# Audio tower on one core: queues written out, gathered rows weighted in one instruction, and another order of pieces

## The chip, the core and the metric

The kernel runs on one core of a Trainium2 chip. A core has TensorE (PE, matmuls into eight PSUM banks), VectorE (DVE), ScalarE (ACT), GpSimd (POOL) and SyncE (SP), each with its own instruction queue and in order; they wait for one another by semaphores. 16 DMA engines move data between HBM and the on-chip SBUF. The metric is the device time of one execution in microseconds (us).

## What is computed

128 sequences of 750 x 64 floats go through a deformable tokenizer (16 taps a word, each read at a computed fractional position), one attention with an additive tanh score, and a mixture of 8 experts of which 2 count, plus a shared expert. Cut to what matters here:

```python
off = jnp.einsum('bwkc,ock->bow', xr, w_off) + b_off[None, :, None]
dy, dx = off[:, 0::2], off[:, 1::2]
px = base[None] + dx;  x0 = jnp.floor(px);  frac = px - x0
wy = jnp.maximum(0.0, 1.0 - jnp.abs(dy))
val = wy[:, None] * ((1.0 - frac)[:, None] * v0 + frac[:, None] * v1)   # v0, v1: rows x0 and x0 + 1
out = jnp.einsum('bckw,dck->bwd', val, w_def) + b_def                    # + class token, positions
h = h + attention(layernorm(h))       # scores + W2 . tanh(hq + hk + b1), softmax
h = h + experts(layernorm(h))         # top 2 of 8, relu, and a shared expert
```

## The kernel before

Work goes in 16 units of 8 sequences. In each unit six sequences take their rows by 36 indirect DMAs of POOL (`gathers`, L382, 128 rows each) into `G`; the other two are read densely: ACT makes hat weights `HT` (pieces `h0`..`h3` for the first of the two, `k0`..`k3` for the second: three Abs instructions of 128x736 at L413, then one Relu of 128x2208 at L420, for each half), and PE multiplies them with the rows `XN` (pieces `n0`..`n3`, L818). Both meet in `VT`, which `b3` (L779) multiplies with the tokenizer's weights.

Each engine's program is a list of short names, `ORDER`; one pass through it is a step. `AHEAD` says how many units ahead of the step a piece works: `t` (turning x, L535) 4 units ahead, `a3`/`a4` (offsets: matmul L793, ACT copy L404, matmul L800, then `stage_a` on DVE from L543) 3 ahead, `h` 2, `k`, `n`, `c`, `b` 1, `m` 0 (first layernorm and attention), `r` one behind (softmax, second layernorm, router), `f`, `g`, `d`, two behind (experts). Expert e is `fe` (PE L940, then ACT relu `HE` L494), `ge` (PE L951 spreads its weight into bank 3, DVE multiplies `GE` L728) and `de` (PE L963). Bank 0 is shared in turn by `a3`, `a4`, `n0` to `n3` and `b3`; bank 2 holds one `f` at a time, bank 3 one `g`.

`c0`, `c1`, `c2` (`combine`, L597 to L618) weight the gathered rows: for each third of a unit a product of 128x768 in place for the first row of every pair, then twice a product of 128x384 into PSUM bank 1 (`prod`) and a sum of 128x384 into `VAL`, and a transpose into `VT`. `stage_a` makes the positions and the indices (`idx`, which POOL waits for) and then, still on DVE, the weights `nw`, `e01` and `aw`. `rstd` is three Newton rounds of three small instructions; `m13` ranks the experts. POOL and SP run their middle part in hardware loops; POOL waits for `idx_ready` of a unit and for `g_free`, counted up by `combine`, before it fills one of two `G` buffers again. SP's list is `x0` (next x), `e0 e1` (the estimates of the tanh score out to HBM), `e2` (back, regrouped, into `SC`, which `r6` of the next step reads), `p0`, `q0` (positions out and back), `y0` (`XN`), `d9` (the store).

## Time and profile before

| | before |
|---|---|
| median of 3 runs | 860.05 us (859.48 to 864.42) |
| the profiled execution | 864.31 us |
| its span, first to last instruction | 862.5 us |
| PE busy | 691.1 us (80%) |
| DVE busy | 670.7 us (78%) |
| ACT busy | 515.8 us (60%) |
| POOL busy | 547.7 us (63%) |
| mean granted TensorE clock | 0.956 |

Busy time is the sum of an engine's instructions; the waits between them are not in it. POOL's gathers have a fixed gap ("issue") between them that is not counted as busy either. The chain that ended last puts 41% of the span on DVE and 37% on PE.

### The profile page before, as it was taken

To read this page: it belongs to the slowest core of one execution; us is meant where nothing else is said; L and a number is where in the kernel's file an instruction comes from. 1 tells how busy PE (TensorE), PEld (TensorE's weight loads), DVE (VectorE), ACT (ScalarE), POOL (GpSimd) and SP (SyncE) were. 2 spreads that over 40 slices of the span, in tenths; PEclk is the share of its full clock that TensorE was granted. 3 is DMA by queue.
4 is the path that set the end of the run, shared out by engine and by line. 5 is a ranking of instruction groups with operands and counts; after the bars stand their busy time and mean duration, and the time that the engine had idled before them with its cause. 6 is when DMAs were issued, how large, how long until landed. Compare 5 with 4: busy or idle time off the path is not lost.

```text
span 862.5 us, 17862 instructions
## 1 busy us (share of the span) xinstructions
PE 691.1 (80%) x6294; PEld 416.1 (48%) x6294; DVE 670.7 (78%) x1750; ACT 515.8 (60%) x903; POOL 547.7 (63%) x588
## 2 busy tenths in 40 slices
PE   2106586879899898989898988888888999998786
PEld 0004354545465555555464645555554555555342
DVE  5146667879888988898898989898888889796552
ACT  0217565647675857767576758585775767744422
POOL 1777777777777777777777777777777777300000
PEclk9999978899989998999999999999999999999889
DMA  4877486647373747565564647475756354200101
GB/s 145 183 180 192 88 170 137 125 84 176 58 206 61 186 86 154 118 123 143 100 169 57 197 76 170 101 155 117 138 131 125 73 93 99 44 18 10 27 0 19
DMA packets 130669, 97.79 MB, mean 113 GB/s; under 512 B 87180, under 2 KB 118868, under 8 KB 130588
## 3 DMA queue, kind: packets, MB, share of 16 engines
q1 hardware_dynamic: 111292, 58.64, 26.3%
q0 software_dynamic: 18432, 37.79, 25.7%
q8 instruction: 50, 0.82, 0.4%
q10 hardware_dynamic: 864, 0.30, 0.1%
q14 instruction: 31, 0.25, 0.1%
HBM read 88.75 MB, written 7.90 MB: 112 GB/s over the span
## 4 chain that ended last, share of the span: by engine, by line
DVE 41%; PE 37%; issue 9%; ACT 5%; SPq 4%; DMA 3%; DVEq 0%; ACTq 0%
PE bank L779 8%; PE bank L940 6%; PE bank L818 5%; DVE XT L535 4%; PE bank L963 4%; DVE bank L609 4%; DVE VAL L615 4%; PE bank L854 3%; DVE G L606 3%; DVE TH L654 3%; DVE VT L632 3%; PE bank L793 2%; DVE GE L728 2%; ACT HT L413 2%; SPq L288 2%
## 5 line engine op out<-in xcount | busy, mean ns | idle before, releaser
L382 POOL DMA_INDIRECT G<-in_x,idx x576 | 545.4, 947 | 195.7 <-issue 173.7
L413 ACT ACTIVATE HT<-PXB,c_lneg 128x736 f32<-128x736 f32 x192 | 160.1, 897 | 74.4 <-PE bank L818 55.5
L818 PE MATMUL bank<-HT,XN 128*32 128x184 f32 x3072 | 137.9, 329 | 8.5 <-ACT HT L420 5.2
L940 PE MATMUL bank<-Z,c_w1e 128*128 128x376 f32 x288 | 125.9, 519 | 20.3 <-ACT HE L494 18.4
L420 ACT ACTIVATE HT<-HT 128x2208 f32<-128x2208 f32 x64 | 130.3, 2036 | 0.6
L818 PEld LDWEIGHTS bank<-HT,XN 128*32 128x32 f32 x3072 | 102.8, 113 | 42.7 <-issue 17.5
L779 PE MATMUL bank<-VT,c_wdef 128*128 128x380 f32 x256 | 87.2, 495 | 23.2 <-DVE VT L632 23.2
L963 PE MATMUL bank<-GE,c_w2e 128*128 128x376 f32 x256 | 104.4, 513 | 0.7 <-DVE GE L728 0.7
L535 DVE STREAM_TRANSPOSE XT<-xt 128x768 f32<-128x768 f32 x64 | 59.9, 958 | 54.2 <-DMA xt<-in_x 33.3
L494 ACT ACTIVATE HE<-bank,c_fb 128x376 f32<-128x376 f32 x128 | 73.0, 570 | 38.9 <-PE bank L940 37.2
L728 DVE TENSOR_TENSOR GE<-HE,bank 128x376 f32<-128x376 f32 x128 | 68.7, 537 | 34.4 <-ACT HE L494 24.7
L779 PEld LDWEIGHTS bank<-VT,c_wdef 128*128 128x128 f32 x256 | 48.1, 193 | 61.5 <-DVE VT L618 28.5
L940 PEld LDWEIGHTS bank<-Z,c_w1e 128*128 128x128 f32 x288 | 49.7, 193 | 57.4 <-ACT HE L494 31.4
L963 PEld LDWEIGHTS bank<-GE,c_w2e 128*128 128x128 f32 x256 | 45.1, 198 | 31.5 <-issue 17.5
L609 DVE TENSOR_TENSOR bank<-G,bank 128x384 f32<-128x384 f32 x96 | 54.0, 562 | 3.3
L615 DVE TENSOR_TENSOR VAL<-G,bank 128x384 f32<-128x384 f32 x96 | 53.1, 553 | 3.3
L793 PE MATMUL bank<-XT,c_wof 128*32 128x384 f32 x256 | 26.5, 536 | 30.3 <-DVE XT L535 20.3
L463 ACT ACTIVATE SC<-SC,smx 47x47 f32<-47x47 f32 x128 | 40.8, 320 | 16.5 <-DVE smx L667 16.5
L618 DVE STREAM_TRANSPOSE VT<-VAL 128x768 f32<-128x768 f32 x48 | 47.0, 978 | 1.7
L606 DVE TENSOR_TENSOR G<-G,bank 128x768 f32<-128x768 f32 x48 | 45.4, 945 | 0.6
L951 PE MATMUL bank<-cT,selb 72*128 72x376 bf16 x128 | 43.5, 340 | 0.3 <-DVE GE L728 0.2
L834 PE MATMUL bank<-h,c_center 128*128 128x376 f32 x64 | 29.1, 536 | 16.7 <-DVE smx L667 16.7
(136 smaller groups left out, 931.3 us busy)
## 6 DMA issues: line engine op xcount, KB each, us to landing
xt<-in_x SPq DMA_DIRECT2D x256, 96.0 KB
PXB<-pw SPq DMA_DIRECT2D x16, 768.0 KB
G<-in_x,idx POOLq DMA_INDIRECT x576
XN<-in_x SPq DMA_DIRECT2D x16, 384.0 KB
est<-SQHC SPq DMA_DIRECT2D x32, 141.0 KB
WYB<-pw SPq DMA_DIRECT2D x64, 48.0 KB
out<-OUTS SPq DMA_DIRECT2D x64, 44.0 KB
SC<-est SPq DMA_DIRECT2D x16, 69.0 KB
```

Of the source, the lines that this page charges most:

```text
L382: pool.indirect_dma_start(out=G[h][:, col, :], out_offset=None, in_=x.rearrange("b (l c) -> (b l) c", c=C), in_offset=bass.IndirectOffsetO ...
L413: act.activation(HT[half][:, c, :, :].rearrange("p g (w n) -> p g w n", n=4), PXB[h][:, :].rearrange("p (g w i n) -> p i g w n", g=NG, i=2 ...
L420: act.activation(rows_, rows_, ACT.Relu, bias=1.0, scale=-1.0).then_inc(hat_ready, 1)
L494: act.activation(HE[e % 4][:, :], cols(2), ACT.Relu, bias=cs["fb1"][:, e:e + 1]).then_inc(he_ready, 1)
L535: dve.transpose(XT[:, :, 96 * bp:96 * bp + 96].rearrange("p q (t i) -> p t q i", i=32), xt[:, WG * bp:WG * bp + WG, :].rearrange("p t (q i ...
L609: ins = dve.tensor_tensor(prod, G[h][:, k0 + a:k0 + b, C:2 * C], weight(1, a, b), ALU.mult)
L615: chain(dve.tensor_tensor(VAL[:, a:b, :], G[h][:, k0 + a:k0 + b, 0:C], prod, ALU.add))
L728: dve.tensor_tensor(GE[e % 4][:, :], HE[e % 4][:, :], cols(3), ALU.mult).then_inc(ge_ready, 1)
L779: mm = pe.matmul(bank[0][:, 0:TOK], wdef[:, q, :], VT[:, q, :], start=(q == 0), stop=(q == KP - 1))
L818: mm = pe.matmul(bank[0][32 * g:32 * g + 32, HW * c:HW * c + HW], XN[h][:, b, C * ch + 32 * c:C * ch + 32 * c + 32], HT[half][:, k, g, :], ...
L940: pe.matmul(cols(2), w1e[:, e, :], Z2[h][:, :], start=True, stop=True).then_inc(up_full, 1)
L963: pe.matmul(cols(4), w2e[:, e, :], HS[:, 0:COLS] if e == E else GE[e % 4][:, :], start=(e == E), stop=False).then_inc(down_done, 1)
```

## The change

- `combine`: one product of 128x1536 in place over both rows of every pair, then one sum of 128x768 that reads both halves of `G` from SBUF and writes `VAL`. The PSUM scratch `prod` is gone; the weights are multiplied out into `awp` at `c0`.
- `stage_a`: the bias of the offsets is added by ACT in `a3`. Abs and Relu that make `nw` and `e01` go to ACT as a new piece `a4` (`row_hats`, five small instructions), `nw` and `e01` are doubled, and the positions are written by SP after ACT's piece.
- `rstd`: 7 small instructions for 9. `m13`: one comparison for two. `m6`: the maximum comes out negated, one instruction less. `dense_out`: a product without the factor -1.
- `ORDER` is another one on all four engines. SP's `y0` stands ahead of `e0 e1 e2`, and `q0` behind the store.
- The loops of SP and POOL are written out. At the start x of unit 0 is issued half by SP and half by ACT, the first constants by POOL ahead of its memsets, the other constants by ACT behind step -3.

```diff
-    "tensor": ("gc n0 fs g0 n1 m0 f0 ds f1 m1 r7 f2 g1 r8 d0 m2 g2 r9 m3 f3 g3 m4 r10 m5 f4 g4 m51 d1 r11 f5 n2 g5 m52 n3 "
-               "r12 d2 f6 g6 d3 b3 f7 g7 a3 d4 a4 d5 d6 d7 d8").split(),
+    "tensor": ("n0 fs gc g0 n1 f0 ds m0 f1 m1 r7 d0 g1 f2 r8 m2 g2 f3 m3 r9 g3 m4 d1 r10 m5 f4 m51 d2 g4 f5 m52 r11 g5 n2 "
+               "f6 r12 g6 d3 f7 g7 d4 d5 n3 d6 b3 d7 d8 a3 a4").split(),
...
-    "sync": ("x0 e0 e1 e2 p0 q0 y0 d9").split(),
+    "sync": ("x0 y0 e0 e1 e2 p0 d9 q0").split(),
...
+        def load_first(eng, parts):
+
+            for bp in parts:
+                src = x[bass.ds(2 * bp, 2), :].rearrange("b (t w g n) -> g w b t n", t=WG, w=16, g=NG)
+                for g in range(NG):
+                    eng.dma_start(xt[32 * g:32 * g + 32, WG * bp:WG * bp + WG, :], src[g]).then_inc(x_in[bp], 16)
...
-            load_x(0, 0)
+            load_first(sp, (0, 1))
...
+            for name, _s in CONSTS[1:NFIRST]:
+                pool.dma_start(cs[name][:, :], consts[name]).then_inc(first_in, 16)
+            pool.dma_start(ident[:, :], consts["ident"]).then_inc(ident_in, 16)
...
-            gathers(0, 0)
-            gathers(0, 1)
-            with pool.Fori(1, UNITS // 2) as i:
-                gathers(i, 0)
-                gathers(i, 1)
+            for u in range(UNITS):
+                gathers(u // 2, u % 2)
...
-                act.activation(off4[:, :], bank[0][:, 0:XCOLS], ACT.Copy).then_inc(off_ready, 1)
+                act.activation(off4[:, :], bank[0][:, 0:XCOLS], ACT.Identity, bias=cs["boff"][:, 0:1]).then_inc(off_ready, 1)
+
+            def row_hats(m, h):
+                u = 2 * m + h
+                act.wait_ge(ot_read, u + 1)
+                if not (isinstance(m, int) and u < 2):
+                    act.wait_ge(pw_out, 6 * 16 * (u - 1))
+                act.activation(nw[h][:, :, :], offT[:, :, 0:4], ACT.Abs).then_inc(nw_abs, 1)
+                act.wait_ge(nw_abs, u + 1)
+                act.wait_ge(rest_ready, u + 1)
+                act.activation(nw[h][:, :, :], nw[h][:, :, :], ACT.Relu, bias=1.0, scale=-1.0).then_inc(pw_ready, 1)
+                for i in range(2):
+                    act.activation(e01[h][:, :, :, i], rest[:, :, :], ACT.Abs, bias=float(i)).then_inc(e_abs, 1)
+                act.wait_ge(e_abs, 2 * u + 2)
+                e = e01[h][:, :, :, :].rearrange("p t n s -> p (t n s)")
+                act.activation(e, e, ACT.Relu, bias=1.0, scale=-1.0).then_inc(e_ready, 1)
...
+            for name, _s in CONSTS[NFIRST + 1:]:
+                act.dma_start(cs[name][:, :], consts[name]).then_inc(const_in, 16)
...
-                chain(dve.scalar_tensor_tensor(nw[:, :, :], offs[:, :, 0:4], -1.0, offs[:, :, 0:4], ALU.mult, ALU.max))
-                dve.tensor_scalar(nw[:, :, :], nw[:, :, :], 1.0, 1.0, ALU.min, ALU.subtract).then_inc(pw_ready, 1)
-                dve.wait_ge(pw_ready, u + 1)
-                chain(dve.scalar_tensor_tensor(e01[:, :, :, 0], rr[:, :, :], ROUND, pxg, ALU.subtract, ALU.subtract))
-                chain(dve.tensor_scalar(e01[:, :, :, 1], e01[:, :, :, 0], 1.0, None, ALU.add))
-                chain(dve.scalar_tensor_tensor(e01f, e01f, -1.0, e01f, ALU.mult, ALU.max))
                 chain(dve.tensor_scalar(rowb[:, :], rowb[:, :], float(NB * LP), None, ALU.add))
-                chain(dve.tensor_scalar(e01f, e01f, 1.0, 1.0, ALU.min, ALU.subtract))
-                chain(dve.tensor_tensor(aw[h][:, :, :, :], e01[:, :, :, :],
-                                        nw[:, 0:GBLK, :].unsqueeze(3).broadcast_to([128, GBLK, 4, 2]), ALU.mult))
...
-                    first = G[h][:, k0:k0 + 2 * n, 0:C]
-                    chain(dve.tensor_tensor(first, first, weight(0, 0, 2 * n), ALU.mult))
-                    for part in range(2):
-                        a, b = n * part, n * part + n
-                        ins = dve.tensor_tensor(prod, G[h][:, k0 + a:k0 + b, C:2 * C], weight(1, a, b), ALU.mult)
...
-                        chain(dve.tensor_tensor(VAL[:, a:b, :], G[h][:, k0 + a:k0 + b, 0:C], prod, ALU.add))
+                    n = 4 * WG
+                    pairs = G[h][:, k0:k0 + n, :].rearrange("p k (s c) -> p k s c", s=2)
+                    chain(dve.tensor_tensor(pairs, pairs, awp[:, k0:k0 + n, :].unsqueeze(3).broadcast_to([128, n, 2, C]), ALU.mult))
+                    dve.tensor_tensor(VAL[:, :, :], pairs[:, :, 0, :], pairs[:, :, 1, :], ALU.add).then_inc(g_free, 1)
+                    dve.wait_ge(g_free, GP * u + bp + 1)
```

What moves on PE is shown where one step passes into the next, which the prediction calls the seam. Before: `b3`'s matmul (L779) stands two rows ahead of the first of these; `a3` (L793) and `a4` (L800) stand among experts' matmuls, then come `gc` (L929) and `n0` (L818).

```order
L951 MATMUL bank<-cT,selb 128x376
L793 MATMUL bank<-XT,c_wof 32x384 x8
L963 MATMUL bank<-GE,c_w2e 128x376
L800 MATMUL bank<-off,c_selm 128x384
L963 MATMUL bank<-GE,c_w2e 128x376 x3
L968 MATMUL bank<-cT,b2s 128x376
L929 MATMUL bank<-identb,c 72x94 x4
L818 MATMUL bank<-HT,XN 32x184 x24
L940 MATMUL bank<-Z,c_w1e 128x376
L951 MATMUL bank<-cT,selb 128x376
L818 MATMUL bank<-HT,XN 32x184 x24
```

In the changed kernel, the same place (line numbers are its own: L736 is `b3`, L920 a `d`, L925 `d8`, L750 `a3`, L757 `a4`, L775 an `n`, L897 an `f`, L886 `gc`, L908 a `g`):

```order
L775 MATMUL bank<-HT,XN 32x184 x24
L920 MATMUL bank<-GE,c_w2e 128x376
L736 MATMUL bank<-VT,c_wdef 128x380 x8
L920 MATMUL bank<-GE,c_w2e 128x376
L925 MATMUL bank<-cT,b2s 128x376
L750 MATMUL bank<-XT,c_wof 32x384 x8
L757 MATMUL bank<-off,c_selm 128x384
L775 MATMUL bank<-HT,XN 32x184 x24
L897 MATMUL bank<-Z,c_w1e 128x376
L886 MATMUL bank<-identb,c 72x94 x4
L908 MATMUL bank<-cT,selb 128x376
L775 MATMUL bank<-HT,XN 32x184 x24
```

`a3` and `a4` now stand side by side with nothing behind them before `n0`, and `g0` comes directly behind `gc`; `n3` stands right ahead of `b3` but for one `d`.

On ACT, at the end of a step, the kernel before had these rows (L457 the estimates, L420 and L413 the hats, L476 the router's Exp, L494 an expert's relu, L404 `a3`, L481 `gc`):

```order
L457 ACTIVATE SQHC<-bank 128x282
L420 ACTIVATE HT<-HT 128x2208
L476 ACTIVATE eg<-lg 94x32
L413 ACTIVATE HT<-PXB,c_lneg 128x736 x3
L494 ACTIVATE HE<-bank,c_fb 128x376
L420 ACTIVATE HT<-HT 128x2208
L494 ACTIVATE HE<-bank,c_fb 128x376
L404 ACTIVATE off<-bank 128x384
L481 ACTIVATE cT<-bank 72x376
```

and the changed kernel these (L447 the router's Exp, L391 and L384 the hats, L465 a relu, L360 `a3`, L367 to L375 the new `a4`, L452 `gc`):

```order
L447 ACTIVATE eg<-lg 94x32
L391 ACTIVATE HT<-HT 128x2208
L384 ACTIVATE HT<-PXB,c_lneg 128x736 x3
L391 ACTIVATE HT<-HT 128x2208
L465 ACTIVATE HE<-bank,c_fb 128x376
L384 ACTIVATE HT<-PXB,c_lneg 128x736 x3
L391 ACTIVATE HT<-HT 128x2208
L360 ACTIVATE off<-bank,c_boff 128x384
L367 ACTIVATE nw<-offT 128x48
L370 ACTIVATE nw<-nw 128x48
L372 ACTIVATE e<-rest 128x36 x2
L375 ACTIVATE e<-e 128x72
```

Five of the eight hat pieces (`k3`, `h0` to `h3`) now stand together ahead of `a3`, with one relu between them.

## Rows read from the trace of the kernel before

**Rows 1.** Busy time by stretch: us, busy of each engine, clock, DMA share, GB/s

```profile
225.03:649.97 424.94, 378.47 (x3539) 230.52 (x3538) 371.01 (x974) 287.99 (x504) 321.30 (x341) 0.97 0.59 128
```

**Rows 2.** Timeline: offT of units 3 and 15, one `c2`

```profile
132.95 0.54 DVE L543 STREAM_TRANSPOSE offT<-bank 128x384 f32<-128x384 f32 x1
696.29 0.58 DVE L543 STREAM_TRANSPOSE offT<-bank 128x384 f32<-128x384 f32 x1 [2.72 <-PE bank L800]
...
767.74 0.94 DVE L606 TENSOR_TENSOR G<-G,bank 128x768 f32<-128x768 f32 x1
```

**Rows 3.** Waits of PE from 411.6 to 459.2: us in total, times, longest

```profile
PE bank L779 <- DVE VT L632: 1.5, 1, 1.5
PE bank L793 <- DVE h L643: 1.3, 2, 0.6
PE bank L834 <- DVE smx L667: 1.2, 1, 1.2
PE bank L940 <- ACT HE L494: 1.0, 1, 1.0
```

**Rows 4.** Timeline of POOL: the first gather and the last of unit 15

```profile
22.42 1.09 POOL L382 DMA_INDIRECT G<-in_x,idx  x1 [19.59 <-DVE idx L551]
...
742.95 0.94 POOL L382 DMA_INDIRECT G<-in_x,idx  x1 [0.30 <-issue]
```

**Rows 5.** Groups by line and form: count, busy us, mean ns, idle before

```profile
L535 DVE STREAM_TRANSPOSE XT<-xt 128x768 f32<-128x768 f32 x64 | 59.9, 958 | 54.2 <-DMA xt<-in_x 33.3 <-PE bank L793 20.5 <-DVE aw L563 0.2
L609 DVE TENSOR_TENSOR bank<-G,bank 128x384 f32<-128x384 f32 x96 | 54.0, 562 | 3.3
L615 DVE TENSOR_TENSOR VAL<-G,bank 128x384 f32<-128x384 f32 x96 | 53.1, 553 | 3.3
L606 DVE TENSOR_TENSOR G<-G,bank 128x768 f32<-128x768 f32 x48 | 45.4, 945 | 0.6
L577 DVE TENSOR_TENSOR diag<-c_ident,ry 94x376 f32<-94x376 f32 x32 | 17.5, 546 | 1.1
L574 DVE SCALAR_TENSOR_TENSOR nt_<-ry 94x4 f32<-94x4 f32 x96 | 15.5, 161 | 3.3
```

**Rows 6.** One `stage_a` from its second instruction, by stretch: us, DVE busy (x)

```profile
415.67:419.08 3.41, 2.99 (x13) 1.00 0.24 61
```

**Rows 7.** Groups by line and form on ACT, and two on PE

```profile
L413 ACT ACTIVATE HT<-PXB,c_lneg 128x736 f32<-128x736 f32 x192 | 160.1, 897 | 74.4 <-PE bank L818 55.5 <-DMA PXB<-pw 18.9
L420 ACT ACTIVATE HT<-HT 128x2208 f32<-128x2208 f32 x64 | 130.3, 2036 | 0.6
L494 ACT ACTIVATE HE<-bank,c_fb 128x376 f32<-128x376 f32 x128 | 73.0, 570 | 38.9 <-PE bank L940 37.2 <-DVE GE L728 1.3
L463 ACT ACTIVATE SC<-SC,smx 47x47 f32<-47x47 f32 x128 | 40.8, 320 | 16.5 <-DVE smx L667 16.5
L818 PE MATMUL bank<-HT,XN 128*32 128x184 f32 x3072 | 137.9, 329 | 8.5 <-ACT HT L420 5.2 <-DVE offT L543 2.6 <-ACT w1pad L515 0.7
L940 PE MATMUL bank<-Z,c_w1e 128*128 128x376 f32 x288 | 125.9, 519 | 20.3 <-ACT HE L494 18.4 <-ACT HS L487 1.8
```

**Rows 8.** Timeline: estimates out and in on SP, and a late read

```profile
448.22 1.06 SPq L326 DMA_DIRECT2D est<-SQHC  x2
454.91 0.28 SPq L333 DMA_DIRECT2D SC<-est  x1
806.71 0.27 SPq L333 DMA_DIRECT2D SC<-est  x1
812.64 0.60 DVE L665 SCALAR_TENSOR_TENSOR SC<-bank,c_b2col,SC 47x376 f32<-47x376 f32 x1 [1.36 <-DMA SC<-est]
```

**Rows 9.** Timeline of the start on SP: x of unit 0, the first late constant

```profile
0.76 10.41 SPq L288 DMA_DIRECT2D xt<-in_x  x16
33.55 0.48 SPq L351 DMA_DIRECT2D c_wdef<-in_wdef  x1
```

**Rows 10.** Timeline of DVE: `c2` of unit 1

```profile
117.58 0.92 DVE L606 TENSOR_TENSOR G<-G,bank 128x768 f32<-128x768 f32 x1
```

More of the change, by code:

```diff
@@ L348, in _ @@
                       "e0": write_estimate(0), "e1": write_estimate(1), "e2": read_estimate}
-            early("sync", pieces, -3)
-            for name, _s in CONSTS[NFIRST + 1:]:
-                sp.dma_start(cs[name][:, :], consts[name]).then_inc(const_in, 16)
-            sp.wait_ge(zeroed, 1)
-            for b in range(NB):
-                sp.dma_start(w2blk[H * b:H * b + H, b:b + 1], rows["w2col"]).then_inc(blk_in, 16)
-            early("sync", pieces, -2)
-            steps(sp, "sync", pieces, last=(UNITS - 6) // 2)
+            steps("sync", pieces, -3, UNITS + 2)
             for h in range(2):
@@ L769, in _ @@
             dve.wait_ge(zeroed, 8)
-            steps(dve, "vector", pieces, chain, loop=False)
+            steps("vector", pieces, -1, UNITS + 2)
         @block.tensor
@@ L991, in _ @@
             pe.wait_ge(setup_mats, 5)
-            steps(pe, "tensor", pieces, loop=False)
+            steps("tensor", pieces, 0, UNITS + 2)
 def kernel(**inputs):
```

156 lines of the change are left out of this document (58 added, 98 removed).

## Prediction, written before the changed kernel was run

> **What bounds the kernel now.** I read the busy time by stretch first. In the nine steps from `offT` of unit 5 to that of unit 14 a step takes 424.94 / 9 = 47.2 us; PE is busy 378.47 / 9 = 42.05 of it, DVE 41.2, ACT 32.0 [rows 1]. No engine is full: PE stands idle 5.2 us a step, and a step cannot go under 42 without less PE work, of which the change takes none. The chain in the table ahead (DVE 41%, PE 37%) says that the two hand the work to and fro.
>
> Next, PE's waits in one step [rows 3]: 1.5 in `b3` for the last transposed row, 1.3 in `a3` for `h0`, 1.2 in `m0` for the softmax maxima (DVE had to get there), 1.0 in `f1` for ACT's relu. Those four are 5.0 of the 5.2. The first three, 4.0 us, are DVE being late, and this is what a lighter DVE can give back.
>
> Then POOL, which its 63% hides. The first gather starts at 22.42 and the last at 742.95 [rows 4]; 575 gathers between them make 720.5 / 575 = 1.253 us each, 45.1 a unit, with next to no waiting. So POOL is a second bound: the last third of unit 15 cannot be combined before its start + 722 and some landing. `c2` of unit 15 runs at 767.74 now [rows 2], 24 us behind POOL's last start. With a step of 47.2 against POOL's 45.1, POOL has slack late in the run; a step under 45.1 would buy nothing more.
>
> **DVE's part.** `combine`: 562 ns against 945 ns for 384 and 768 columns is 1.0 ns a column [rows 5], so the product of 1536 takes 0.945 + 0.77 = 1.71, the sum of 768 0.95, together 2.66 against 0.945 + 2 x 0.562 + 2 x 0.553 = 3.18. With two gaps less it saves 0.6 a third, 1.8 a unit. `stage_a`: 13 instructions in 3.41 [rows 6], of which six stay: 1.8 less. `rstd`: twice two instructions of 0.161 and their gap of 0.03, 0.8. `m13` and `m6`: one instruction of 256 columns (0.4 by the same 1.0 ns a column) and one small, 0.6. Sum: 5.0 of DVE's 41.2 a step, 80 us over 16 units. The bound from below for the sum with both inputs in SBUF is the 0.553 x 2 of today's halves; from above I come to it as a rival.
>
> **ACT's part.** Five small instructions a unit, each between 0.16 (L574) and 0.32 (L463) [rows 5, 7]: 1.2. ACT had 15 us to spare a step. They stand behind `a3`, where ACT would wait for `gc` anyway; `gc` gets its turn about 2.5 after `offT`, when PE reaches it too. I cost them at nothing; were PE not still in `n0`, it would be up to 1.2 a step.
>
> **The step after.** DVE's 5.0 only counts where PE waits for DVE, so I go through PE's waits in the new order, with durations of the rows.
> 1. `a3`, `a4`, `n0` follow each other on bank 0, and no expert's matmul covers them any more (the seam in the order rows). After `a3`, ACT copies (0.5, like L494's 0.57 [rows 7]) and `a4` follows; after `a4`, DVE transposes (0.54 [rows 2]) and `n0` follows. With 0.15 of latency each, an estimate: 0.7 + 0.7 = 1.4.
> 2. `g0` comes directly behind `gc` and waits for ACT's copy of `cT`: 0.5.
> 3. `f1` waits for ACT's relu of `f0`, which is behind the eight Exps of `r6`. From the end of `offT`: the rest of `stage_a` 1.6, four transposes 4 x 0.958 less overlap = 3.7 [rows 5], sum and maximum 1.2, eight Exps at 0.32 = 2.6, relu 0.57 [rows 7]: 9.7. PE has `n0 fs gc g0 n1 f0 ds m0` in it: two dense pieces at 137.9 / 64 = 2.15, four of the size of L940 at 125.9 / 144 = 0.87 less 0.15 of overlap each [rows 7], `gc`, `g0` and the 0.5 of point 2: 8.1. Wait 1.6.
> 4. `f2` waits for the relu of `f1`, which ACT does behind `k0` (3 x 0.897 less overlap = 2.4 [rows 7]) and two copies: 3.6 after `f1` starts, PE has 2.9 in it: 0.7.
> 5. `b3` waits for `dense_out` of `n3` (0.8 and latency) with one `d` beside it: 0.3.
> 6. From `f2` to `n3` I find PE with work throughout: DVE, 5 us lighter, reaches `diag`, `GE` and `VT` ahead of it.
>
> Sum 4.5 against 5.2 today. So the reordering and the lighter DVE remove the waits for `VT`, `h0` and the maxima, and lay bare a seam that was covered. A step becomes 42.05 + 4.5 = 46.5, 0.7 less. The twelve steps from `offT` of unit 3 (132.95) to unit 15 (696.29) [rows 2] give 8.4.
>
> **Start.** x of unit 0 takes SP 10.41 us for 16 issues [rows 9]; on two queues it is there some 5 earlier. But DVE also waits for the first constants, and POOL issues them now, six at about a gather's 1.25: 7.5 and the landing, which eats a part of the 5. Unit 0's offsets then no longer stand behind x of unit 1. I take the first gather at 20.3 (18.5 if POOL's issues are quick, 22 if slow). The constants that began at 33.55 on SP [rows 9] are issued by ACT from about 21, and x of unit 2 is not behind them. So the setup comes ten earlier and POOL becomes the limit: `c2` of unit 1 no earlier than 20.3 + 72 x 1.253 + 1.5 = 112, now 117.58 [rows 10]. I take 6 for the start.
>
> **End.** Behind unit 15's offsets the steps are chains of latency; two `rstd` (0.4 each), one ranking, one `combine` and a maximum lie on them, and DVE reaches the softmax sooner: 3, with 0 and 6 as bounds, as the order of pieces changes too.
>
> **Sum.** 6 + 8.4 + 3 = 17.4. The profiled execution took 864.31, which is 0.5% over the median of 860.05; 864.3 - 17.4 = 846.9, times 860.05 / 864.31 is 843.
>
> **Rivals.**
> - *POOL is the limit (chance 0.18).* If the waits of points 3 and 4 are shorter, the step falls to 45.1 and POOL never stops. `c2` of unit 15 then comes at 20.3 + 722 + 1.5 = 744, 24 earlier, and 3 at the end: 837, or 833. For it: DVE has 11 us a step to spare. Against: points 3 and 4 are ACT's chain, not DVE's.
> - *The step gains nothing (0.22).* ACT has five hat pieces in a row ahead of `a3`: three Relus of 2.0, two triples of 2.4 and a relu, 11.5 [rows 7], against 13 on PE from `g6` to the end of `a3`. 1.4 of slack; if ACT comes to `k3` 2 later than I think, each step is 0.7 longer and stays at 47.2. The same comes out if the estimate is late: `y0` now holds SP until `dense_out` of this step, so `e0`, `e1`, `e2` follow it; issue to issue 6.7, and 5.9 from `e2` to the sum that waits for it [rows 8], 13.5 with `y0`, against 15 until `r6`. Only start and end are left: 864.3 - 9 = 855, or 851 to 858.
> - *The sum from memory to memory disturbs POOL (0.07), slower.* Today each large product or sum of `combine` has one side in PSUM. If each new sum of 0.95 holds up one gather, or waits for one, POOL needs 45.1 + 3 x 0.95 = 48.0 a unit; its last gather starts at 788, `c2` of unit 15 at 790 for 767.74: 864.3 + 22 - 3 = 883, or 879. It decides from 2.2 us a unit on. Against it: `diag` has both inputs in SBUF, and its 546 ns for 376 columns lie on the same line as the products with PSUM (0.562 for 384) [rows 5], and POOL's pace of 1.253 leaves no room for held gathers [rows 4]. The Trainium skill (SBUF — State Buffer, Who interferes with whom) says that a DVE instruction with two SBUF inputs contends with a GpSimd instruction that reads SBUF, and only with such a one; the gather reads its indices there. By that rule the time is this rival's; the rows of today do not show it.
> - *The seam is dearer (0.05).* Should `a3` to `n0` cost 3.5 in place of 1.4, the step is 48.6: 864.3 - 9 + 17 = 872, or 868.
>
> **Chances.** The forecast (838 to 850) has 0.48. Faster by over 1%, about what a measurement of this kernel can tell, is under 851.4: the forecast, POOL's case and a third of the no-gain case, with a little off for what I have not seen, 0.70. Within 1%: 0.19. Slower: 0.11, the last two rivals. The range from 832 to 859 holds the first three cases.
>
> **What would show it.** `offT` to `offT` in the middle: 46.5 (45.1 for POOL, 47.2 for no gain). DVE busy down to about 590. The product of 1536 at 1.71, the sum at 0.95; POOL's gather still 0.947 and its gap 0.3. First gather at 18.5 to 22. PE's waits for ACT at `f1` and `f2`, and for `off` and `offT` at the seam, in place of those for `VT`, `h` and `smx`. Wrong I would be if PE's busy time moved, if DVE waited for gathers in the middle of the run, or if SP's estimate ended a wait in every step.

## The result and the profile after

| | before | after |
|---|---|---|
| median of 4 executions | 862.23 us (859.48 to 865.72) | 852.97 us (846.73 to 856.24) |
| the profiled execution | 864.31 us | 846.73 us |
| `offT` of unit 0 to that of unit 3 | 113.2 us | 112.7 us |
| twelve steps, `offT` of unit 3 to that of unit 15 | 563.3 us | 552.9 us |
| `offT` of unit 15 to the end | 166.2 us | 160.1 us |

The ratio is 0.989 (0.986 to 0.992): 1.1% faster, where 2.0% was forecast. The profiled execution of the changed kernel is the quickest of its four, that of before one of its slower ones; the pair differs by 17.6 us, the medians by 9.3. The table's last three rows are read from the two profiled executions.

Busy time, from the page of the changed kernel:

```profile
PE 692.2 (82%) x6294; PEld 407.5 (48%) x6294; DVE 607.0 (72%) x1399; ACT 534.9 (63%) x983; POOL 562.6 (67%) x594
```

DVE is down by 63.7 us (80 forecast), PE as it was, POOL up by 15. Nine steps by stretch, to be set beside [rows 1]:

```profile
224.31:639.20 414.89, 378.07 (x3537) 222.45 (x3537) 336.57 (x774) 298.44 (x549) 315.23 (x328) 0.98 0.67 129
```

and PE's waits in the same stretch (us in total, times, longest):

```profile
PE bank L897 <- ACT HE L465: 14.9, 14, 2.2
PE bank L757 <- ACT off L360: 6.8, 9, 0.8
PE bank L775 <- DVE offT L520: 6.1, 9, 0.7
PE bank L908 <- ACT cT L452: 5.1, 9, 0.6
PE bank L736 <- DVE VT L594: 2.3, 9, 0.3
```

A step is 414.89 / 9 = 46.1 us, 1.1 less than in [rows 1]; over the twelve steps of the table it is 46.08 for 46.95, 0.9 less. PE is busy 42.0 of it as before, and its waits have changed places: those of [rows 3] for `h` and `smx` and most of that for `VT` are gone; in their place stand the seam (`off` 0.76, `offT` 0.68), the copy `cT` 0.57, and ACT's relu 1.66 a step.

POOL's group of gathers (count, busy, mean ns, idle before them and what ended it):

```profile
L343 POOL DMA_INDIRECT G<-in_x,idx x576 | 556.9, 967 | 190.0 <-issue 174.3 <-DVE idx L527 15.1 <-DVE VAL L576 0.6
```

and, to be set beside [rows 4], its first two gathers and its last one:

```profile
21.53 1.01 POOL L343 DMA_INDIRECT G<-in_x,idx  x1 [14.76 <-DVE idx L527]
22.84 0.98 POOL L343 DMA_INDIRECT G<-in_x,idx  x1 [0.30 <-issue]
...
752.73 0.94 POOL L343 DMA_INDIRECT G<-in_x,idx  x1 [0.30 <-issue]
```

Of 190.0 us idle between gathers, 174.3 are the 0.30 of issue and 14.8 the wait before the first. POOL never stops otherwise. From first to last it needs 731.2 / 575 = 1.272 us a gather, for 1.253 before: a gather takes 967 ns on average, 947 before. The last third of units 1 and 15 on DVE ([rows 10] and [rows 2] of before):

```profile
115.59 1.75 DVE L575 TENSOR_TENSOR G<-G,bank 128x1536 f32<-128x1536 f32 x1 [3.21 <-DMA G<-in_x,idx]
756.38 1.75 DVE L575 TENSOR_TENSOR G<-G,bank 128x1536 f32<-128x1536 f32 x1 [0.64 <-DMA G<-in_x,idx]
```

and the shares of the chain that ended last:

```profile
POOL 39%; PE 22%; issue 15%; DVE 8%; DMA 7%; ACT 7%; SPq 2%; POOLq 0%; ACTq 0%; DVEq 0%
```

In both places DVE waits for a gather. Before, the last third of unit 15 ran 24.8 us behind the start of POOL's last gather; now it runs 3.7 behind it, and POOL leads the chain where DVE and PE did.

One thing has to be said for what follows: on several of the later occasions every execution with all the gathers issued one behind the other, of the kernel before too, took near 1570 us; a section further down shows what happens in them. r1 to r10, r15 and r16 were measured on such occasions, r11 to r14, r17 and r18 on others, where the kernel before took near 862. A ratio is always to the kernel before on the same chip and occasion.

### The profile page after: what moved, and what is told of

Same layout as the page of the kernel before. It is cut to its first block, busy times and chain, and to the rows that moved or that the text cites. A ratio compares the mean times of both kernels' runs of the same rounds, so it can differ in the third digit from the quotient of the medians.

```text
span 844.9 us, 17031 instructions
## 1 busy us (share of the span) xinstructions
PE 692.2 (82%) x6294; PEld 407.5 (48%) x6294; DVE 607.0 (72%) x1399; ACT 534.9 (63%) x983; POOL 562.6 (67%) x594
## 4 chain that ended last, share of the span: by engine, by line
POOL 39%; PE 22%; issue 15%; DVE 8%; DMA 7%; ACT 7%; SPq 2%; POOLq 0%; ACTq 0%; DVEq 0%
POOL G L343 39%; PE bank L736 4%; PE bank L897 4%; PE bank L775 3%; PE bank L920 3%; ACT HT L384 2%; ACT SC L434 2%; DVE XT L511 2%; DMA SC<-est 1%; DMA est<-SQHC 1%; DMA G<-in_x,idx 1%; DMA PXB<-pw 1%; SPq L253 1%; ACT HT L391 1%; PE bank L869 1%
## 5 line engine op out<-in xcount | busy, mean ns | idle before, releaser
L343 POOL DMA_INDIRECT G<-in_x,idx x576 | 556.9, 967 | 190.0 <-issue 174.3
L384 ACT ACTIVATE HT<-PXB,c_lneg 128x736 f32<-128x736 f32 x192 | 159.8, 897 | 28.0 <-DMA PXB<-pw 21.9
L775 PE MATMUL bank<-HT,XN 128*32 128x184 f32 x3072 | 139.8, 334 | 24.4 <-DVE offT L520 9.4
L897 PE MATMUL bank<-Z,c_w1e 128*128 128x376 f32 x288 | 128.8, 530 | 28.0 <-ACT HE L465 26.6
L775 PEld LDWEIGHTS bank<-HT,XN 128*32 128x32 f32 x3072 | 98.5, 114 | 71.0 <-DVE offT L520 18.6
L391 ACT ACTIVATE HT<-HT 128x2208 f32<-128x2208 f32 x64 | 130.4, 2038 | 1.2
L465 ACT ACTIVATE HE<-bank,c_fb 128x376 f32<-128x376 f32 x128 | 72.6, 567 | 69.9 <-PE bank L897 52.8
L920 PE MATMUL bank<-GE,c_w2e 128*128 128x376 f32 x256 | 106.0, 510 | 0.0
L736 PE MATMUL bank<-VT,c_wdef 128*128 128x380 f32 x256 | 87.2, 495 | 9.4 <-DVE VT L594 9.4
L575 DVE TENSOR_TENSOR G<-G,bank 128x1536 f32<-128x1536 f32 x48 | 84.0, 1750 | 5.4 <-DMA G<-in_x,idx 4.8
L897 PEld LDWEIGHTS bank<-Z,c_w1e 128*128 128x128 f32 x288 | 47.9, 195 | 72.2 <-ACT HE L465 46.0
L736 PEld LDWEIGHTS bank<-VT,c_wdef 128*128 128x128 f32 x256 | 48.3, 193 | 47.6 <-issue 14.3
L511 DVE STREAM_TRANSPOSE XT<-xt 128x768 f32<-128x768 f32 x64 | 57.1, 947 | 1.3 <-DMA xt<-in_x 0.7
L520 DVE STREAM_TRANSPOSE offT<-bank 128x384 f32<-128x384 f32 x16 | 9.3, 583 | 66.3 <-PE bank L757 66.3
L920 PEld LDWEIGHTS bank<-GE,c_w2e 128*128 128x128 f32 x256 | 43.9, 193 | 24.7 <-issue 13.8
L908 PE MATMUL bank<-cT,selb 72*128 72x376 bf16 x128 | 42.8, 334 | 9.1 <-ACT cT L452 9.1
L576 DVE TENSOR_TENSOR VAL<-G 128x768 f32<-128x768 f32 x48 | 46.1, 960 | 1.6
L750 PE MATMUL bank<-XT,c_wof 128*32 128x384 f32 x256 | 26.5, 536 | 23.3 <-DVE XT L511 20.4
L757 PE MATMUL bank<-off,c_selm 128*128 128x384 f32 x32 | 15.3, 563 | 36.8 <-ACT off L360 36.8
```

Source lines behind the costliest of these rows:

```text
L343: pool.indirect_dma_start(out=G[h][:, col, :], out_offset=None, in_=x.rearrange("b (l c) -> (b l) c", c=C), in_offset=bass.IndirectOffsetO ...
L384: act.activation(HT[half][:, c, :, :].rearrange("p g (w n) -> p g w n", n=4), PXB[h][:, :].rearrange("p (g w i n) -> p i g w n", g=NG, i=2 ...
L391: act.activation(rows_, rows_, ACT.Relu, bias=1.0, scale=-1.0).then_inc(hat_ready, 1)
L465: act.activation(HE[e % 4][:, :], cols(2), ACT.Relu, bias=cs["fb1"][:, e:e + 1]).then_inc(he_ready, 1)
L511: dve.transpose(XT[:, :, 96 * bp:96 * bp + 96].rearrange("p q (t i) -> p t q i", i=32), xt[:, WG * bp:WG * bp + WG, :].rearrange("p t (q i ...
L575: chain(dve.tensor_tensor(pairs, pairs, awp[:, k0:k0 + n, :].unsqueeze(3).broadcast_to([128, n, 2, C]), ALU.mult))
```

## The experiments

Two theories stood against each other. **A**: POOL with its 576 gathers sets the changed kernel's time, and the new sum from SBUF to SBUF makes the gathers longer. **B**: the engines' own step sets it (seam and ACT's chain, as the forecast has it), and POOL stays hidden.

### r1: the changed kernel again

> The changed kernel once more, to see what its executions have in common. Its profiled execution took 846.7, three others 852.7 to 856.2. Theory A (POOL is the limit of this kernel, and how long its gathers are held varies from one execution to the next): the median is 852 to 853, and a second profile shows POOL without a stop from 21.5 on, with gathers longer than 0.95 us beside the sum L576, mean 960 to 985 ns; the longer the gathers in all, the longer the time. Theory B (the engines' step is the limit and the gathers merely keep up): the gathers take the same 556.9 us in all, or another sum that the time does not follow, and combine waits for no gather.

1568.39 us, 0.9986 of the kernel before (0.9962 to 1.001), which itself took 1572.17. Neither the times nor the 1.1% of the first measurement came back; POOL's mean gather was 958 ns. What executions of this kind can tell is how a change weighs in the part of a step that doesn't stand still.

### r2 and r5: the combine of before

Told in short (the names are the kernel's, the lines are not its own words):

```diff
-pairs = pairs * awp                       # one product, 1536 columns, in place
-VAL = pairs[..., 0, :] + pairs[..., 1, :]  # one sum, both inputs in SBUF
+first = first * w0                        # 768 columns
+for part in range(2):
+    prod = second[part] * w1              # 384 columns, into PSUM bank 1
+    VAL[part] = first[part] + prod        # 384 columns
```

> The changed kernel with the five products and sums of the kernel before in combine (one side of each large one in PSUM), all else as changed. DVE gets 0.5 to 0.6 us a third more, 1.8 a unit, of the 11 it has to spare. Theory A (the sum with both inputs in SBUF holds POOL's gathers, and POOL is the limit): the gathers go back to 945 to 950 ns, the last starts about 11 us earlier, and the time falls by 4 to 9 us against the changed kernel, to 844 to 849. Theory B (the step of PE, DVE and ACT is the limit): the time stays at 853 or rises by what the 1.8 us lay on the path, up to 858.

> The changed kernel with the five products and sums of the kernel before in combine, on another chip if it is given: in the four runs ahead of this one every execution of every kernel, that of before too, took 1565 to 1596 us, with ACT standing still for about 45 us once a step (12 such waits, 546 us), so they can't tell the theories apart. Theory A (the sum with both inputs in SBUF holds POOL's gathers, and POOL is the limit): gathers back to 945 to 950 ns, 844 to 849 us against 853 of the changed kernel. Theory B (the step of PE, DVE and ACT is the limit): 853 to 858.

1.0121 of before (1.0094 to 1.0148), and on another chip 1.0098 (1.0081 to 1.0115): by these ratios 1.4% and 1.1% over r1. Gathers fell to 952 and 950 ns. There DVE's own time is what counts, and the shorter gathers give nothing back. The old combine in the new order was not measured with all gathers near 862.

### r3: SP's read of rows later

```diff
-    "sync": ("x0 y0 e0 e1 e2 p0 d9 q0").split(),
+    "sync": ("x0 e0 e1 e2 y0 p0 d9 q0").split(),
```

> The changed kernel with y0 (the load of XN) moved on SP from ahead of e0 e1 e2 to behind them. The changed kernel's r6 waited 8.2 us in all for the estimate to come back. If those waits lie on the path (the step is the limit): 3 to 6 us faster than the changed kernel, 847 to 850. If POOL is the limit (theory A), the middle of the run gains nothing, and only the waits of the last two steps (3.3 and 1.9 us) can: 850 to 853. The waits of L627 for the estimate are to vanish in the middle either way.

0.9998 (0.9979 to 1.0018), r1's time. That the estimate comes too late behind `y0` is not what a step is made of. In the first profile too DVE waited for it only six times, 8.2 us in all.

### r4: the kernel before with the new order

The four lists of `ORDER` of the changed kernel in the kernel before (ACT's without `a4`, a piece it doesn't have there).

> The kernel before with the four lists of the changed kernel and nothing else (its stage_a stays whole on DVE, so ACT's a4 is left out). Prediction's account (the lighter DVE is needed for the new order: with DVE 5 us heavier, stage_a and four transposes stand at the seam ahead of r6, so the wait of f1 grows by 1.8 and r6 by as much): a step of 48 to 49 us, 862 to 885, slower than before. Rival (the order alone carries the gain): 850 to 856, as the changed kernel.

1.0111 of before (1.0084 to 1.0138): in executions of this kind the new order by itself makes the kernel before slower.

### r6: the sum twice

```diff
+chain(dve.tensor_tensor(VAL, pairs[:, :, 0, :], pairs[:, :, 1, :], ALU.add))
 dve.tensor_tensor(VAL, pairs[:, :, 0, :], pairs[:, :, 1, :], ALU.add).then_inc(g_free, 1)
```

> The changed kernel with the sum L576 issued twice (the second writes the same values again): 0.96 us more of DVE a third, 2.9 a unit, all of it with both inputs in SBUF. Theory A (that sum holds POOL's gathers): the time that gathers of over 1.0 us have beyond 0.944 doubles, and the mean gather goes from 967 to about 980 ns; where POOL is the limit the time is 6 to 11 us above the changed kernel. Theory B (the gathers are held by something else): the gathers stay at 967, and the time rises by 0 to 8 us from DVE's 2.9 a unit alone.

1.0116 (1.0079 to 1.0154), 1.3% over r1. 46 us more of DVE cost some 20 us of time; the mean gather went from 958 to 962 ns only. In these executions the engines mostly stand still while gathers are issued, so sum and gather seldom meet (29 gathers of r6 overlap a sum, 70 in the changed kernel's first profile). This run does not tell the two theories apart.

### r7 to r9: three gathers a unit

```diff
-for k in range(4 * WG):     # 12 gathers in each third
+for k in range(1):
```

> The changed kernel with one gather in each third of a unit in place of twelve (48 in all for 576). G is zeroed once by POOL and the combine runs on it at full size, so the output is not the reference's; DVE, ACT, PE and SP have all their work. On the chips of r1 to r6 ACT and PE stand still some 45 us a step while POOL issues its 36 gathers. Theory G (it is the gathers that hold them): with three gathers a unit the standstills go, the time falls from about 1570 to about 850. Theory other (clock or something else of those chips): it stays above 1400. If the gathers go, the step shows the engines' own limit. Theory A (POOL is what limits the changed kernel's step of 46.1): the step falls below 45.1, to 44 to 45 us, and the time to 820 to 835. Theory B (the seam and ACT's chain limit it): the step stays at 46.0 to 46.3 and the time at 840 to 850.

> The kernel before with one gather in each third of a unit in place of twelve, G zeroed once, all other work kept; output not the reference's. Theory G: the standstills go and the time falls to about 860. POOL had slack in the kernel before (step 46.95 for 45.1 of gathers), so both A and B expect 46.7 to 47.0 a step and 855 to 862. Against r7 theory B expects a ratio of 0.98 to 0.99 (what was measured with all gathers, 0.989), theory A 0.955 to 0.97.

> As r7, with the order of pieces of the kernel before (a4, which ACT must run, behind a3). Output not the reference's. Separates the order from the lighter instructions in the engines' own step. If the order of the change is what turns DVE's 5 us into a shorter step, this one is slower than r7 by 0.5 us a step or more, 6 us and up. The forecast's points 1 and 2 put 1.9 us of new waits on the new order and took 4.0 us of old ones away by the lighter DVE alone, which by itself would make this one faster than r7, by up to 1.5 a step. I expect r9 slower than r7 by 1%, as r4 showed the orders to matter by that much.

The kernel before took 1566.99 beside them. r7: 854.1 us. r8: 879.9. r9: 839.5. So the gathers are what makes the 1570: with one in twelve left, the time halves. And r9, the changed kernel's instructions in the order of before, is 1.7% quicker than r7, where 1% slower was expected. Even three gathers still held ACT: in nine steps of r8 and of r9,

```profile
ACT HT L417 <- remote: 45.0, 9, 5.1
```

```profile
ACT HT L388 <- remote: 37.3, 9, 4.4
```

("remote" is a releaser that the trace can't name), so the ratio of r7 to r8 is no clean answer to A or B. That needed kernels with no gather at all.

### r10: POOL pauses ahead of each third

```diff
+if u or bp:
+    q = GP * u + bp - 1     # the third before this one
+    pool.wait_ge(gathered[q // GP % 2][q % GP], 16 * 4 * WG * (q // GP // 2 + 1))
```

> The changed kernel, but POOL waits ahead of each third (twelve gathers) until the third before has landed, a pause of 3.6 to 4 us each, 11 to 12 a unit; nothing left out. Theory G1 (ACT and PE are held as long as gathers follow each other without stop, from the first on): they get on with their work in each pause, the standstill of 45 us breaks into three of 12 to 15, and the time stays within 2% of r1's 1568. Theory G2 (they are held only once a number of gathers is under way): the pause takes that away and the time falls by 200 us or more. Theory N (the pause doesn't let them go on): 12 x 11 us more, 1700.

1390.1 us, 0.886 of before (0.883 to 0.890). A step fell from 93.0 to 82.0 us although POOL now stands still until every twelve gathers have landed. G2 wanted 200 us or more, 177 came. ACT's standstills in one step, from its timeline:

```profile
572.02 0.57 ACT L468 ACTIVATE HE<-bank,c_fb 128x376 f32<-128x376 f32 x1 [8.92 <-remote]
581.38 0.48 ACT L419 ACTIVATE Y<-bank 128x376 f32<-128x376 f32 x1 [8.79 <-remote]
...
589.14 0.60 ACT L409 ACTIVATE V<-bank 128x512 f32<-128x512 f32 x1 [4.79 <-remote]
```

One of 45 us has become several of 5 to 9. Pauses let PE and ACT on.

### r11 to r14: no gathers

`G` is zeroed once, POOL issues nothing, all the rest of the work stays.

> The changed kernel with no gathers at all: G is zeroed once by POOL and the combine runs on it at full size; all the work of DVE, ACT, PE and SP is kept, the output is not the reference's. Three gathers a unit still left PE 11.2 us of holes without a releaser in nine steps of r7 (1.2 a step) and ACT 13.5; these should go. Theory A (POOL and its gathers set the changed kernel's step): 44.9 to 45.2 a step. Theory B (the engines set it, gathers cost nothing): 46.0 to 46.4. The time is then 830 to 840 or 845 to 855.

> The kernel before with no gathers, G zeroed once, all other work kept; output not the reference's. In r8 ACT stood 45.0 us at the hats with a releaser that the trace does not show, 5.0 a step, and PE 11.1 behind it; without gathers this goes. The engines' own step of the kernel before, expected at 46.9 by both theories (it had 1.8 us of slack to POOL's 45.1), time 855 to 865; ratio r11 / r12 by B 0.985 to 0.99, by A 0.96 to 0.975.

> The changed kernel's instructions in the order of the kernel before, no gathers; output not the reference's. By r9 against r7 (839.5 and 854.1) the new order costs 1.7%. If that came from where the held instructions stand and not from the order as such, r13 equals r11 within 0.3%. If the order itself costs, r13 is 0.5 to 1 us a step quicker, 830 against 845. I expect the latter, with a step of 45.0.

> The changed kernel with the combine of before (four halves, products through a PSUM bank), no gathers; output not the reference's. DVE is 1.8 us a step dearer. With all gathers it was 1.3% slower than the changed kernel (r2, and 1.1% by r5). If that is DVE's own time on the path, it is so here too: 0.8 to 1.3% over r11. If the combine only counted through the gathers (held ones, or G freed later), it is within 0.3% of r11.

The kernel before took 861.19 beside them.

| no gathers | time, us | ratio to before (with its gathers) | step, mean of 12 |
|---|---|---|---|
| r12 kernel before | 853.4 | 0.9892 (0.9858 to 0.9927) | 46.64 |
| r11 changed kernel | 843.8 | 0.9791 (0.9753 to 0.9829) | 45.66 |
| r14 changed kernel, old combine | 863.5 | 1.0016 (0.9991 to 1.0042) | 46.67 |
| r13 changed kernel, old order | 798.8 | 0.9265 (0.9235 to 0.9294) | 42.66 |

None of the four is quite what had been expected: r11's step lies between A's 44.9 to 45.2 and B's 46.0 to 46.4, r12 is just under its 855 to 865, r13 was put at 830 us, and r14 is 2.3% over r11 for 0.8 to 1.3 expected.

The same nine steps, by stretch and then PE's waits. r11:

```profile
226.01:635.34 409.33, 375.37 (x3537) 220.90 (x3537) 333.33 (x775) 298.54 (x549) 0.00 (x0) 0.99 0.31 79
```

```profile
PE bank L895 <- ACT HE L463: 12.4, 17, 0.8
PE bank L755 <- ACT off L358: 6.8, 9, 0.8
PE bank L773 <- DVE offT L518: 6.1, 9, 0.7
PE bank L906 <- ACT cT L450: 5.1, 9, 0.6
PE bank L734 <- DVE VT L592: 2.3, 9, 0.3
```

r13:

```profile
207.99:593.58 385.59, 369.51 (x3539) 227.23 (x3538) 327.93 (x775) 294.24 (x549) 0.00 (x0) 0.99 0.33 84
```

```profile
PE bank L895 <- ACT HE L463: 8.9, 9, 1.0
PE bank L748 <- DVE h L603: 5.7, 9, 0.6
PE bank L836 <- DVE TH L614: 0.7, 3, 0.2
```

Four things follow. (1) Changed kernel against kernel before: 843.8 / 853.4 = 0.989 without gathers, as with them, and a step is 1.0 us shorter for 0.9 with them. The engines' own step carries most of the difference, as B says; by the medians the gathers cost both kernels some 9 us. The times are a little unfair to r11, r13 and r14: with `G` being zeroed, their first `offT` comes at 23.5 us, for 19.2 in the changed kernel and 19.8 in r12. The steps don't have this flaw. (2) All of the change but the order (r13 against r12) takes 4.0 us off a step and 55 off the time. (3) Without gathers the new order gives 3.0 of those 4.0 and 45 of the 55 us back. Its five waits are 32.7 / 9 = 3.6 us a step where the old order leaves 15.3 / 9 = 1.7, and PE's busy time in r13 is 0.65 a step lower. (4) The in-place combine is worth 1.0 a step and, by the medians, 20 us in this order, for 1.3 us of DVE's busy time a step (11.7 us in the nine steps, r14 against r11).

### r15 and r17: the changed kernel with the old order, all gathers

```diff
-    "tensor": ("n0 fs gc g0 n1 f0 ds m0 f1 m1 r7 d0 g1 f2 ...
-               "... f7 g7 d4 d5 n3 d6 b3 d7 d8 a3 a4").split(),
+    "tensor": ("gc n0 fs g0 n1 m0 f0 ds f1 m1 r7 f2 g1 ...
+               "... d3 b3 f7 g7 a3 d4 a4 d5 d6 d7 d8").split(),
```

(The other three lists likewise, with `a4` behind `a3` for ACT.)

> The changed kernel with the order of pieces of the kernel before (a4, which ACT must run, behind a3); all 576 gathers, nothing left out. Without gathers this order made a step of 42.66 us against 45.66 of the changed kernel (r13, r11). If the executions are of the kind of the first measurement (kernel before near 862): theory A, POOL is the limit as soon as the engines are quicker: POOL starts at about 21.5 and issues 576 gathers at 1.25 to 1.27, so its last third lands at 745 to 757, 86 to 88 us of tail follow, 832 to 845 in all, and a step is 45.1 to 45.8 with DVE waiting for gathers. Theory B, gathers cost the engines no time: 42.7 to 43.5 a step is impossible beyond POOL's pace, so it would show only as 835 and DVE never waiting. In either case faster than before by 2 to 3.5%. If they are of the kind of r1 (near 1570): 1540 to 1560, as the new order alone cost 1.1% there (r4).

> The kernel of r15 once more (changed kernel, order of pieces of the kernel before, nothing left out), because r15 and its kernel before ran near 1570. If the kernel before is near 862 here: by theory A 832 to 845, 0.965 to 0.98 of it, with DVE waiting for gathers at the first third of most units and a step of 45.1 to 45.8; if the gathers left no trace the 42.66 of r13 would give 800, which POOL's 576 gathers at 1.25 rule out. If the kernel before is near 1570 again: 0.987 as r15.

r15: 0.987 (0.984 to 0.990) beside executions near 1570. r17, with the kernel before at 862.1: 856.8 us, 0.9934 (0.9901 to 0.9966). Faster than before, but above the 0.965 to 0.98 that A had given, and no quicker than the changed kernel (0.989, measured on another occasion): with all gathers the new order gives nothing back. Of the 55 us that this order had without gathers 5 are left. The chain that ended last, and two groups, of r17:

```profile
POOL 55%; issue 19%; PE 10%; DMA 6%; DVE 5%; ACT 3%; SPq 1%; POOLq 0%; DVEq 0%; ACTq 0%
```

```profile
L343 POOL DMA_INDIRECT G<-in_x,idx x576 | 557.9, 969 | 191.4 <-issue 174.3 <-DVE idx L527 16.4 <-DVE VAL L576 0.6
...
L575 DVE TENSOR_TENSOR G<-G,bank 128x1536 f32<-128x1536 f32 x48 | 83.9, 1748 | 36.9 <-DMA G<-in_x,idx 36.3
```

Here POOL is the limit: 55% of the chain, no stop between gathers, and 36.3 us in which DVE stands waiting for them, in eleven places from unit 1 to unit 15 (4.8 in the changed kernel). A step is 45.89 us; POOL needs 36 x (0.969 + 0.30) = 45.7 a unit. Whatever the engines could save under that is lost.

### r16 and r18: old order and old combine

The edits of r15 and r2 together.

> As r15, but the combine of the kernel before (four halves a third through a PSUM bank) in place of one product in place and one sum from SBUF to SBUF; nothing left out. DVE has 1.8 us a step more to do, and the gathers no sum with both inputs in SBUF beside them. If POOL is the limit in r15 and that sum holds gathers up (mean 967 ns against 947, 20 ns x 576 = 11.5 us), this one is 5 to 11 us FASTER than r15, with gathers back at 947 to 952 ns. If DVE's time is what counts, it is 8 to 16 us slower (1.0 a step by r14 against r11). Near 1570: 1.0 to 1.3% slower than r15, as r2 was against r1.

> The kernel of r16 once more (changed kernel with the order of pieces and the combine of the kernel before, nothing left out), since r16 ran near 1570 where gathers hold PE and ACT. In r17 POOL ran from 22.90 to 756 without a stop (576 gathers of 969 ns and 0.30 between them) and DVE waited for gathers. If the kernel before is near 862 here: by theory A the sum from SBUF to SBUF is what makes gathers 969 instead of 947 ns, so here they are back at 947 to 952 and POOL ends 10 to 12 us earlier; the engines' step without gathers is about 43.7 (42.66 plus the 1.0 that the old combine cost in r14), still under POOL's 45.1; the time falls from r17's 0.993 of before to 0.975 to 0.985, 841 to 849, a version quicker than both. If DVE's time decides, it rises by 1.0 a step, 1.01 of before. If the gathers stay at 965 to 970 ns without that sum, something else in the new kernel holds them, and the ratio is 0.99 to 1.00. Near 1570 again: 0.999 as r16.

r16: 0.9993 (0.9978 to 1.0007) near 1570, 1.2% over r15: DVE's time counts there. r18, with the kernel before at 862.1: **845.0 us, 0.9797 (0.9774 to 0.9821)**, 1.4% under r17, with 21.5 us MORE of DVE busy time. POOL in r18, its group and its first and last gather:

```profile
L344 POOL DMA_INDIRECT G<-in_x,idx x576 | 547.2, 950 | 191.5 <-issue 174.6 <-DVE idx L528 16.6 <-DVE bank L583 0.3
```

```profile
23.05 1.01 POOL L344 DMA_INDIRECT G<-in_x,idx  x1 [16.27 <-DVE idx L528]
...
744.56 0.94 POOL L344 DMA_INDIRECT G<-in_x,idx  x1 [0.31 <-issue]
```

Without the sum from SBUF to SBUF the gathers take 10.7 us less in all, the last one starts 10.6 us sooner than it did in r17 (755.12), and the median falls by 11.8, the profiled execution by 6.5. DVE's waits for gathers go from 36.3 to 3.7 us:

```profile
DVE G L580 <- DMA G<-in_x,idx: 3.7, 2, 1.9
```

This version is quicker than both kernels: 2.0% under the kernel before, where the changed kernel is 1.1% under it.

POOL's pace is not the whole of it, though. The twelve steps take 550.0 us in r18 and 550.7 in r17; what the profiled pair gains it gains behind `offT` of unit 15 (162.5 for 168.7), where `c2` of r17 still waits 5.1 for a gather. In r18 POOL needs only 36 x (0.950 + 0.30) = 45.0 a unit and DVE waits for no gather after the first few units, and yet a step is 45.83, not the 43.7 that had been put down for its engines:

```profile
222.51:639.69 417.18, 384.85 (x3539) 236.19 (x3538) 344.42 (x857) 294.87 (x549) 315.98 (x333) 0.95 0.60 130
```

PE is busy 42.8 us of a step here, at a granted clock of 0.95, and 41.1 at 0.99 in r13. So gathers seem to cost the old order some 2 us a step also where nothing waits for them, an estimate, since this version was not run without gathers. By what way was not tried.

## Why the forecast was off, by its own steps

Two steps of the forecast failed. The term for the start, 6 us, came to 1.1. And the last step, which carried a saving worked out on one profiled execution over to the median, did not hold: the profiled pair moved by 17.6 us, the medians by 9.3. The account term by term:

**What bounds the kernel, right.** PE's 42 us and the waits around it; r12 shows the engines' step of before at 46.64 without a gather.

**DVE's part, right but for size.** The product took 1.75 us (1.71 forecast), the sum 0.96 (0.95). DVE's busy time fell by 64, not 80; part of that is the gaps between instructions, which the 80 held and busy time doesn't (351 instructions fewer, some 10 us at the forecast's 0.03 each, an estimate).

**ACT's part at nothing, right.** PE waits for no hat in those nine steps, and behind `a4` it is ACT that waits for PE's `gc`:

```profile
ACT cT L452 <- PE bank L886: 10.9, 9, 1.3
```

**The step, right.** 46.1 measured for 46.5 forecast, and nearly term by term: seam 1.43 (1.4), `g0` 0.57 (0.5), ACT's relu at the `f` pieces 1.66 (2.3), `b3` 0.26 (0.3). The twelve steps gave 10.4 us for 8.4. (The 8.4 was more than its own step allowed: the 0.7 was taken off the 47.2 of nine steps, while these twelve average 46.95, and twelve of 46.5 save 5.) What the forecast did not do is to cost the same lighter instructions in the OLD order. r13 did it without gathers: 42.66. The seam and ACT's chain were counted as the price of a gain, and they were larger than what the order brought there.

**The start, wrong: 6 forecast, 1.1 measured at `offT` of unit 3.** The sum itself had said that POOL becomes the limit here, with `c2` of unit 1 no earlier than 20.3 + 72 x 1.253 + 1.5 = 112. It came at 115.59, after a wait of 3.21 for its gather: the first gather was 1.2 late (21.53), the 72nd started at 111.26, 0.8 later than at 1.253 each, and `c2` ran 4.3 behind that start where the sum allowed 2.8. The landing of the last gather of unit 15 is 3.62 us in the chain. All three terms were taken on the short side, and so `c2` of unit 1 gained 2.0 us where 6 had been taken. The gathers are not all of it. From `offT` of unit 0 to that of unit 3:

| | all gathers | no gathers |
|---|---|---|
| kernel before | 113.2 | 108.0 (r12) |
| changed kernel | 112.7 | 109.0 (r11) |
| changed kernel, old order | 112.2 (r17) | 101.9 (r13) |

So with no gather to wait for, the changed kernel takes no less time for these three steps than the kernel before does; the new order costs it 7.0 us against the old one, 4.6 of them in the step from unit 2 to unit 3 (43.9 and 39.3). That price of the order in the first steps is in no term of the forecast.

**The end, right in sign: 3 forecast, 6.1 measured** (4.8 between r12 and r11).

**From the profiled execution to the median, wrong.** The sum of 846.9 for the profiled execution met 846.73, but by luck: 1.1 + 10.4 + 6.1 in place of 6 + 8.4 + 3, from a slower execution of one kernel to the quickest of the other. Executions of the changed kernel spread over 9.5 us, as much as the whole gain; the medians moved by 9.3. Without gathers the pair of medians moved by 9.7 (853.43 to 843.78). So the saving is near 10 us, and the forecast of 17 was some 8 too much. The start explains 5 of them at most, and in which steps the other executions are longer than the profiled one is open, since only one is profiled. Their granted clock is not lower (0.946 to 0.952, for 0.937 in the quickest).

**The rival that the memory-to-memory sum disturbs POOL (0.07): its mechanism is real, its size a quarter.** It put 2.85 us on a unit's 45.1; measured are 20 ns more a gather, 0.7 a unit, 11.5 us in all. One held gather, in the changed kernel's timeline of POOL and DVE:

```profile
625.32 0.94 POOL L343 DMA_INDIRECT G<-in_x,idx  x1 [0.30 <-issue]
626.56 1.69 POOL L343 DMA_INDIRECT G<-in_x,idx  x1 [0.30 <-issue]
...
626.47 0.96 DVE L576 TENSOR_TENSOR VAL<-G 128x768 f32<-128x768 f32 x1
627.47 0.98 DVE L580 STREAM_TRANSPOSE VT<-VAL 128x768 f32<-128x768 f32 x1
```

The gather starts 0.09 behind the sum and ends 0.82 behind the sum's end, 0.75 longer than its neighbour; the product L575 ahead of it has its weights in PSUM, and of the 56 gathers that overlap it, but neither the sum nor the small product L569, none takes over 0.96. Of 70 gathers that overlap the sum 22 are longer, by 7.7 us together; the other 48 are not, so it takes the right moment of a gather. Another 26 long gathers, 5.5 us together, run beside no such sum. Nine of them overlap the ranking's comparison L656 and five the product L569, both small and both with two SBUF inputs; the kernel before has 13 long ones in all, 1.7 us. r17 and r18 are the proof for the sum: with it taken away, 969 becomes 950 ns and the time falls by 1.4%, on two chips whose kernel before took the same 862.1. The Trainium skill (SBUF — State Buffer, Who interferes with whom) says that a DVE instruction with two SBUF inputs contends with a GpSimd instruction that reads SBUF. This case's trace agrees in kind (967 to 969 ns with that sum, 947 to 950 without); how much to expect had to be measured. The forecast dismissed it with two arguments that could not carry that: DVE's `diag` is not longer with two SBUF inputs [rows 5] says nothing of POOL, which is the side that was held; and a steady pace of 1.253 [rows 4] was the pace of a kernel that had no such sum of that size.

**The rival that POOL is the limit (0.18): true in part, and it hid what mattered.** At 45.8 a unit for POOL (36 x 1.272) against 45.66 a step for the engines (r11) the changed kernel has both limits at the same place. POOL's 45.1 did hold as a floor with all gathers: no version's step went under 45.8. It does not explain the miss, though, since the kernel before gains about as much from leaving the gathers out (r12) as the changed one (r11). What gathers took away is what the old order had to give: 798.8 without them, 856.8 with them.

## What happens in the executions near 1570 us

Each step of 93 us holds the step of 46 and one standstill. In r1, stretches of one step (PE, weight loads, DVE, ACT, POOL busy; granted clock):

```profile
330.00:341.00 11.00, 7.96 (x115) 4.08 (x113) 7.09 (x19) 2.74 (x9) 3.36 (x4) 1.00 0.30 24
341.00:352.00 11.00, 6.71 (x14) 2.13 (x14) 4.27 (x5) 2.43 (x16) 8.54 (x9) 0.69 0.82 171
352.00:370.00 18.00, 0.43 (x1) 0.00 (x0) 0.00 (x0) 0.00 (x0) 13.45 (x15) 0.55 0.45 120
370.00:385.00 15.00, 0.00 (x0) 0.00 (x0) 0.00 (x0) 0.00 (x0) 9.19 (x10) 0.50 0.20 48
```

and where it begins and ends, in the timelines of POOL, PE and ACT:

```profile
336.73 0.94 POOL L343 DMA_INDIRECT G<-in_x,idx  x1 [47.89 <-DVE idx L527]
...
344.06 0.49 PE L775 MATMUL bank<-HT,XN 128*32 128x184 f32 x1 [0.95 <-issue]
351.96 0.48 PE L791 MATMUL bank<-h,c_center 128*128 128x376 f32 x1 [0.87 <-issue]
...
388.38 0.57 ACT L465 ACTIVATE HE<-bank,c_fb 128x376 f32<-128x376 f32 x1 [44.95 <-remote]
```

POOL issues its 36 gathers from 336.7 to 381.9 at the usual pace. Some 4 us after the first, PE begins to show holes that no releaser explains, 0.4 us at first and 0.95 three us later, when it is down to one small matmul at a time, and then PE, ACT and DVE all stand until 6.5 us after the last gather. ACT's relu had its input from PE by about 349.4 and ran at 388.38. TensorE's granted clock falls from 1.00 to 0.50, from 2.4 to 1.2 GHz, while it has nothing to do. r7 and r8 show that the gathers bring it about, r10 that pauses between them let the others on. What in a gather holds the other engines, and why only on some occasions and on the same chip (r1 and r11 ran on the same one), is open: packets of instructions are fetched at 336.8, 337.3 and 345.6 us and then not before 400.2, after the engines have started again, which neither shows nor rules out that they starve. It also hid the question: in those executions gathers and engines take turns, so POOL is no limit beside them, and only DVE's and PE's own time shows (r2, r4, r5, r6, r16 all cost 1.1 to 1.4% over the kernel they change).
